# Issuing attention scores one slot sooner on TensorE, and projecting v right behind k, in the third of four cross-attention blocks

## The reference

```
def attention(q, k, v, mask):
    scores = jnp.einsum('bhqd,bhkd->bhqk', q, k) / jnp.sqrt(jnp.float32(HD))
    scores = scores * mask - 10000.0 * (1.0 - mask)
    probs = jax.nn.softmax(scores, axis=-1)
    return jnp.einsum('bhqk,bhkd->bhqd', probs, v)
ln_out = layernorm(hidden_states, ln1_s, ln1_b)
qkv = ln_out @ w_qkv + b_qkv
q, k, v = jnp.split(qkv, 3, axis=-1)
ctx = merge_heads(attention(split_heads(q), split_heads(k), split_heads(v), ltor_mask))
x = hidden_states + ctx @ w_ao + b_ao
ln_out = layernorm(x, ln2_s, ln2_b)
q = ln_out @ w_q + b_q
k, v = jnp.split(encoder_states @ w_kv + b_kv, 2, axis=-1)
ctx = merge_heads(attention(split_heads(q), split_heads(k), split_heads(v), cross_mask))
x = x + ctx @ w_co + b_co
ln_out = layernorm(x, ln3_s, ln3_b)
return x + gelu(ln_out @ w1 + b1) @ w2 + b2
```

## Time and profile before

| | |
|---|---|
| median of 3 runs | 1594.3 us (1592.65 to 1597.76) |
| the profiled execution's own time | 1595.42 us |
| its span | 1593.6 us |
| busy: PE, DVE, ACT, POOL | 1489.5, 934.5, 907.3, 144.6 us |
| stretch 1080 to 1320 us (third block's attention): PE, DVE, ACT busy | 201.37, 219.66, 203.72 of 240 us |
| mean granted TensorE clock over the span | 0.978 |

### The profile page before, as it was taken

How to read it: one execution, slowest core, us unless ns; L and a number is a source line. 1 busy time by engine, 2 the same in 40 slices (tenths; PEclk the granted TensorE clock), 3 DMA queues, 4 the chain that set the end, 5 groups by cost and what they waited for, 6 DMA issues and landing times. The chain is left out here.

```text
span 1593.6 us, 28683 instructions
## 1 busy us (share of the span) xinstructions
PE 1489.5 (93%) x9824; PEld 1147.4 (72%) x9824; DVE 934.5 (59%) x3314; ACT 907.3 (57%) x2807; POOL 144.6 (9%) x163
## 2 busy tenths in 40 slices
PE   7999999999999999999999999997897888988886
PEld 5666687888787787778787878785665657866554
DVE  4777624545454455545554555318989992278886
ACT  5788824444443443444444434337888884398885
POOL 2000010000000001000000000101222311012200
PEclk9999999999999999999999999998999999999998
DMA  7000103010100101001010000001001000000000
GB/s 285 2 2 2 62 1 119 1 47 15 47 15 1 61 1 61 1 1 61 1 61 1 1 0 1 1 1 54 1 2 41 9 8 7 1 4 6 22 4 12
DMA packets 10879, 40.66 MB, mean 26 GB/s; under 512 B 2416, under 2 KB 2672, under 8 KB 8688
## 3 DMA queue, kind: packets, MB, share of 16 engines
q1 hardware_dynamic: 10736, 38.82, 6.9%
HBM read 37.77 MB, written 1.05 MB: 24 GB/s over the span
## 5 line engine op out<-in xcount | busy, mean ns | idle before, releaser
L943 ACT ACTIVATE probs<-probs,negmax 128x256 f32<-128x256 f32 (+1 forms) x640 | 347.2, 548 | 77.8 <-DVE negmax L1186 77.4
L1017 ACT ACTIVATE pT<-bank 128x512 f32<-128x512 f32 x128 | 76.4, 597 | 388.0 <-PE bank L761 388.0
L558 PEld LDWEIGHTS bank<-ident,probs 128*128 128x128 f32 x1536 | 178.6, 147 | 95.0 <-issue 44.2
L558 PE MATMUL bank<-ident,probs 128*128 128x128 f32 x1536 | 233.8, 290 | 10.0 <-DVE pT L1194 6.3
L1309 DVE TENSOR_REDUCE stats<-bank 128x1 f32<-128x257 f32 x256 | 108.4, 425 | 212.3 <-PE bank L753 211.3
L1186 DVE CUSTOM_DVE_ANT_0 probs<-bank,mask_a 128x256 f32<-128x256 f32 (+1 forms) x384 | 178.4, 508 | 50.4 <-PE bank L545 42.1
L951 ACT ACTIVATE pT<-bank 128x512 f32<-128x512 f32 x288 | 168.8, 587 | 25.6 <-PE bank L558 25.3
L545 PE MATMUL bank<-kT,q_res 32*128 32x256 f32 (+1 forms) x1280 | 112.6, 458 | 36.6 <-DVE negmax L1186 29.3
L772 PE MATMUL bank<-pT,probs 128*128 128x256 f32 x512 | 132.7, 381 | 2.7 <-ACT pT L1017 2.7
L753 PE MATMUL bank<-kT,pT 128*128 128x257 f32 x512 | 132.7, 382 | 0.6 <-ACT pT L1000 0.6
L943 ACT ACTIVATION_READ_ACCUMULATOR probs<-probs,negmax 128x1 f32 x640 | 124.8, 195 | 0.0
(11 more groups left out here) (110 smaller groups left out, 2490.6 us busy)
## 6 DMA issues: line engine op xcount, KB each, us to landing
w_m<-in_w SPq DMA_DIRECT2D x6, 1024.0 KB, 6.9
g_qkv<-in_g SPq DMA_DIRECT2D x4, 1536.0 KB, 6.9
q_res<-in_g SPq DMA_DIRECT2D x4, 1536.0 KB, 6.7
w_qkv<-in_w SPq DMA_DIRECT2D x3, 768.0 KB, 4.3
g_bv<-in_gbv SPq DMA_DIRECT2D x8, 256.0 KB, 7.0
g_o<-in_go SPq DMA_DIRECT2D x4, 512.0 KB, 3.4
q_res<-in_go SPq DMA_DIRECT2D x4, 512.0 KB, 3.5
rows<-in_rows SPq DMA_DIRECT2D x1, 1664.0 KB, 14.3
```

The lines of the kernel that those rows point to most:

```text
L558: last = nc.tensor.transpose(out[:, n * P:(n + 1) * P], probs[:, u % PROBS, q * T + t * P:q * T + (t + 1) * P], ident[:, :])
L943: last = nc.scalar.activation(s, s, ACT.Exp, bias=negmax[:, u % PROBS, k:k + 1], scale=-1.0, accum_out=sums[:, tile % 2, q, j * c.res + r: ...
```

## The change

`Small` gets a parameter `ahead`, which is 1 for the third block and 0 for the other two. TensorE then issues `scores(u)` in slot u-1 instead of u, but for the first quad. Within the slot, scores stand first, so they now precede one more unit's transposes and whatever else ends slot u-1. For the kinds "mult", which only the third block has, the projection of v for the next part begins in slot 8 instead of 13. With it moves the evacuation of v on VectorE (to slot 8), and the order of uses of bank 7 becomes norm rows 0, q 3, k 6, v 8, y 10. Nothing is added or removed; ScalarE's, GpSimd's and SyncE's orders are the same as before, and so is VectorE's but for v.

```diff
@@ class Small
-                 vector_copies=(), host=None):
+                 vector_copies=(), host=None, ahead=0):
...
+        self.ahead = ahead
...
-        at = [3, 6, 13] if self.kinds == "mult" else [2, 6, 14] if len(self.loads()) == 3 else [2, 6, 14, 22, 26]
+        at = [3, 6, 8] if self.kinds == "mult" else [2, 6, 14] if len(self.loads()) == 3 else [2, 6, 14, 22, 26]
...
-          scale=0.25, turn_lag=5, copy_lag=3, host="l21"),
+          scale=0.25, turn_lag=5, copy_lag=3, host="l21", ahead=1),
@@ TensorE
                 def slot(s):
-                    if s < c.count and s % QUAD == 0:
-                        if s % c.units == 0:
-                            p, n = s // c.units, [w for w in c.loads() if w[0] == "k"][-1]
+                    u = s + c.ahead if s else 0
+                    if u < c.count and u % QUAD == 0:
+                        if u % c.units == 0:
+                            p, n = u // c.units, [w for w in c.loads() if w[0] == "k"][-1]
...
-                        scores(s)
+                        scores(u)
```

## The result

The changed kernel takes 1604.85 us (median of 4 runs, 1603.81 to 1611.45), the kernel before 1593.47 (1591.76 to 1597.76): 11.4 us more, a ratio of 1.0083 with a 95% interval of 1.0064 to 1.0101. The forecast was 1602, slower. The profiled execution is the slowest of the four (1611.45, span 1609.7). Its stretch from the first v evacuation to the next stage's first product is 12.0 us longer than before; the other 4.0 us lie ahead of that stretch, in code that is the same in both.

A forecast was written before the change was run, and what follows sets the result against it. VectorE, busy 219.66 of 240 us, was taken to bound the stretch. A longer TensorE chain and the other parts gave +4.4 us, the low clock +3.5: +7.9, so 1602 us, range 1588 to 1611.

The forecast's parts named there:

- M to Y: Per part, end of first quad's masks until VectorE needs y's second half; before, 99.3 us over parts 1 to 6.
- Y to Y: One whole part, between VectorE's needs for y's second half: 31 to 32 us forecast, 30.9 before.
- Y to M: From VectorE needing y's second half to the end of the next first quad's masks: 0.8 us shorter without v.
- M to Y of 18.1: Parts 1 to 6: TensorE's 17.2 us of work, 0.8 wait at v, 0.1 hand-over before VectorE's add.
- the 1.4 us for transposes and half of q: TensorE work formerly ahead of the second quad's scores, now behind them: one unit's transposes and q's first half.
- the 9.9 us: Time from the second quad's scores until TensorE reaches v: 8.0 plus 1.4 moved in plus 0.5 for one unit.
- The term for the fourth quad's scores, 1.1: These scores stood behind y and now precede its second half on TensorE, adding 1.1 us.
- Part 0, +0.7: The reciprocals' 1.8 us wait can go, early v adds waits: between -1.8 and +2.5 us, taken as +0.7.
- The clock, +3.5: Low TensorE clock reaching past the first quad's masks: 0.7 us in five parts, bounds 0 and 2.4 each.
- A: VectorE's waits for TensorE go, nothing replaces them: 13.7 us gained, 1581, or 1586 partially; chance 0.14.
- B: Added wait at v for k's evacuation doesn't bite: total about -0.4 us plus little clock, 1594 to 1597; chance 0.20.
- C: Low clock reaches past the first quad's masks in every part, 2.4 us six times: 1613; chance 0.13.

The follow-up runs named there:

- The changed kernel with the added activation: Changed kernel plus one 128 x 256 ScalarE activation (about 0.36 us) per part ahead of q's evacuation: 1604.38 us, ratio 1.0076.

## Why the prediction was right, point by point

- *Slower, because M to Y grows and y comes late.* Right: VectorE's wait for y grew from 0.55 to 2.61, Y to Y is 31.7 us where I said 31 to 32, and the fourth quad's scores alone, put back, return 11.3 us.
- *What goes.* Right: the norm rows' wait is down to 1.0 us and VectorE's waits for scores to 1.7 of 8.0, both of them in part 0; Y to M is 0.79 shorter, as counted (0.8).
- *M to Y of 18.1.* Measured 18.64, and 19.5 in part 1. Summed over the six parts 8.6 us instead of 4.5. The tail from v to y was right (1163.19 to 1170.61, 7.4; counted 7.3). The start of v was not: I took ScalarE's k at 10.7 behind M from a part where it ran without waits, and missed that the third quad's scores, moved as well, hold back the transposes that ScalarE needs (by the timelines): 11.06, and with it a wait of 1.08 instead of 0.8. And the 1.4 us for transposes and half of q are in the 9.9 us, but cost nothing.
- *The term for the fourth quad's scores, 1.1.* 1.23 measured, and it acts in part 7 too, where I had credited 0.8 and got 0.
- *Part 0, +0.7.* Measured 3.5 (from the first v evacuation to M of part 1: 36.9 us before, 40.3 after). In VectorE's timeline of the changed kernel v waits 2.07 and the reciprocals 3.13 where 1.8 stood:

```profile
1103.64 0.88 DVE L1145 TENSOR_TENSOR v_two<-bank,rows 128x128 f32<-128x128 f32 x4 [2.07 <-PE bank L531]
...
1114.91 0.43 DVE L1217 COPY recipT<-bank 128x256 f32<-128x256 f32 x1 [3.13 <-PE bank L589]
```

About half of it is the low clock of this execution. The changed kernel with the added activation has the same TensorE list in part 0 and takes 38.5 us there, 1.8 less. TensorE stands 1.65 us ahead of the same times-v in both, first in the changed kernel, then in the other, where the reciprocals wait 1.68 us:

```profile
1111.55 1.86 PE L581 MATMUL bank<-pT,v_two 128*32 128x256 f32 x16 [1.65 <-ACT pT L953]
```

```profile
1107.90 1.07 PE L583 MATMUL bank<-pT,v_two 128*32 128x256 f32 x16 [1.65 <-ACT pT L957]
```

- *The clock, +3.5.* Wrong in its place. In parts 2 to 7 the low level comes only ahead of M; in part 0, for which I had no such term, it cost the 1.8. Four stretches of the changed kernel, with parts 4 and 5 inside the last:

```profile
1144.00:1150.00 6.00, 5.43 (x48) 4.32 (x48) 5.97 (x22) 4.15 (x14) 1.38 (x1) 0.72 0.01 1
1150.00:1176.00 26.00, 20.97 (x192) 14.95 (x184) 22.22 (x79) 22.58 (x74) 6.05 (x7) 1.00 0.01 2
1176.00:1180.00 4.00, 3.79 (x26) 3.17 (x27) 3.90 (x14) 1.97 (x6) 1.38 (x1) 0.57 0.00 0
1180.00:1272.00 92.00, 73.17 (x684) 52.38 (x686) 80.22 (x288) 78.19 (x254) 22.32 (x25) 1.00 0.05 19
```

Parts 2 and 3 have such a stretch ahead of their M, parts 4 and 5 none, and M to Y is 18.64 in all four: idle time takes it up entirely. The stand that TensorE takes behind y, before the next part's first scores, is 2.45 us ahead of each of the parts 2 to 7. Behind it these scores run slowly ahead of part 3 (1.83 us at 1176.21, shown above) and at full speed ahead of part 4:

```profile
1207.94 1.15 PE L546 MATMUL bank<-kT,q_res 32*128 32x256 f32 x16 [2.45 <-DVE probs L1170]
```

The Trainium skill ("TensorE: Matmul & The Clock Gate", Part 1, what's actually happening) says that the default state is throttled and activity releases the throttle. The trace agrees in part: the clock fell behind the new stands, as it had behind the old one, but not behind each. What it costs depends on where it falls.
- *The rivals.* A (the waits go and nothing replaces them) fell: the wait for y took their place. B (no wait at v) fell: the wait is 1.08. C (clock on the chain) fell.

So the total was near (7.9 against 12.0 in the profile and 11.4 between the medians) partly by luck: part 0, part 7 and parts 1 to 6 were each set too low, by 2.8, 0.8 and 4.1, and the clock's 3.5, which came to 1.8 in another place and is part of these 2.8, stood against that. My cause also pointed at both halves of the change. The six kernels with v in 13, 8 or 12, without and with the sooner scores, show that only one half costs:

| v in slot | 13 | 8 | 12 |
|---|---|---|---|
| scores in their old slots | 1593.5 | 1593.3 | 1581.9 |
| scores one slot sooner | 1603.9 | 1604.9 | 1594.3 |

What stays open: the other 1.7 us of part 0, and the 2 to 3 us between the sooner scores' prices with v in 13 and in 12.

## What to carry to other kernels

An operation that is moved up is moved ahead of something. Before moving it, ask of each instance what its consumer waits for now, and what the consumer of the one it overtakes waits for: here three quads of four gained little, and the fourth overtook the one product on which the busiest engine already waited. When a stand is caused by one buffer's release, move that release by the smallest step that clears it, to a place where the path has room (v from 13 to 12, 12 us), and not to the earliest possible place.

Read a chain across all engines from the kernel that will run, not from a part where one engine happened to run freely, and price the low clock only where its stretch lies on the chain.

## What the runs showed of the hardware that was not expected

Y to M is 13.32 us with v in slot 12 and 13.87 with v in slot 13, though VectorE does the same instructions in it. The difference is one of its reductions (L1186 before, L1188 in the other), which runs beside GpSimd's bias add. In the kernel before, part 2, VectorE and then GpSimd:

```profile
1165.15 1.48 DVE L1186 CUSTOM_DVE_ANT_0 probs<-probs,mask_a 128x256 f32<-128x256 f32 x1
```

```profile
1164.97 1.38 POOL L1422 TENSOR_TENSOR x_rows<-x_rows,rows 128x512 f32<-128x512 f32 x1 [3.59 <-DVE y_rows L1099]
```

It takes 1.48 us instead of 0.42 and ends 0.28 us behind GpSimd's add. With v in 12, v's evacuation, which reads PSUM and one operand in SBUF, lies beside the start of that add and takes 0.88 us as elsewhere; the reduction behind it takes 0.92:

```profile
1167.17 0.92 DVE L1188 CUSTOM_DVE_ANT_0 probs<-probs,mask_a 128x256 f32<-128x256 f32 x1
```

```profile
1166.54 1.27 POOL L1424 TENSOR_TENSOR x_rows<-x_rows,rows 128x512 f32<-128x512 f32 x1 [3.59 <-DVE y_rows L1101]
```

The reduction again ends 0.28 us behind that add (1168.09 against 1167.81).

So 0.5 us of the 2.4 that a part gains in that kernel come from what runs beside GpSimd. The Trainium skill ("SBUF — State Buffer", who interferes with whom) has the shared port pair of VectorE and GpSimd as an exclusive lock; these rows agree, for a VectorE operation with two inputs in SBUF.
